# Row maxima inside the last value projections, the values of a head in one group, and three banks for scores, in an attention and mixture-of-experts layer

## What is computed

```python
q = _split_heads(hidden_states @ Wq + bq)   # 2 batches, 16 heads of 32
k = _split_heads(hidden_states @ Wk + bk)
v = _split_heads(hidden_states @ Wv + bv)
ctx = _local_attention(q, k, v)             # 8 blocks of 128 queries, each over 256 keys around it
idx = _global_index(q)                      # token 0, the 62 largest |q|, token 1023
qg = jnp.take_along_axis(q, idx[..., None], axis=-2)
g_scores = jnp.einsum('nhqd,nhkd->nhqk', qg, k) / math.sqrt(d)
g_ctx = jnp.einsum('nhqk,nhkd->nhqd', jax.nn.softmax(g_scores, axis=-1), v)
ctx = ctx.at[bn, bh, idx].set(g_ctx)
...
x = x + _layernorm(_L0_attn_ref(_layernorm(x), ...))
x = x + _layernorm(_L0_ffn_ref(_layernorm(x), ...))   # 8 experts, top 1, and a shared expert
```

## Time and profile before

| what | value |
|---|---|
| median of 3 runs (lowest, highest) | 936.01 us (935.06, 940.03) |
| profiled execution: its time | 939.68 us |
| profiled execution: its span | 937.9 us |
| PE busy | 854.9 us, 91% |
| DVE busy | 579.7 us, 62% |
| ACT busy | 412.6 us, 44% |
| mean granted PE clock | 0.957 of full speed |

### The profile page before, as it was taken

One profiled execution on the slowest core, in us unless ns is written; L12 is line 12 of the kernel. 1 busy time (PEld: TensorE's weight loads), 2 busy tenths in 40 slices (PEclk: granted clock), 3 DMA queues, 4 the chain that ended last, 5 costly groups with the idle time before them and its releaser, 6 DMA issues.

```text
span 937.9 us, 13768 instructions
## 1 busy us (share of the span) xinstructions
PE 854.9 (91%) x5094; PEld 681.8 (73%) x5094; DVE 579.7 (62%) x1236; ACT 412.6 (44%) x771; POOL 135.8 (14%) x189
## 2 busy tenths in 40 slices
PE   3999999978899899999879999989999999999995
PEld 2676776756566666666658778779999999877773
DVE  5636994668745554656448754436666677648565
ACT  2523241215446555555544424346666666633120
POOL 4000003020030000111113552100000000012222
PEclk9999999969989999999979889989999999999997
DMA  6696554973656855762025862256666667645434
GB/s 202 180 331 193 165 158 143 268 198 90 183 153 170 199 130 159 185 195 79 14 70 195 277 230 82 89 161 206 209 210 203 201 212 208 209 134 164 156 124 134
DMA packets 116642, 161.07 MB, mean 172 GB/s; under 512 B 17156, under 2 KB 65028, under 8 KB 116576
## 3 DMA queue, kind: packets, MB, share of 16 engines
q1 hardware_dynamic: 112992, 152.23, 53.8%
q0 software_dynamic: 3584, 7.97, 3.0%
HBM read 105.93 MB, written 55.05 MB: 172 GB/s over the span
## 4 chain that ended last, share of the span: by engine, by line
PE 75%; DVE 13%; ACT 5%; DMA 3%; issue 2%; POOL 1%; SPq 1%; DVEq 0%; POOLq 0%
PE bank L162 43%; PE wide L162 24%; PE wide L166 4%; PE bank L166 3%; DVE SG L159 2%; ACT PG L156 2%; DMA H<-scr_oe,FG 1%; DMA scr_v<-vt 1%; DVE XT L148 1%; DVE STC L266 1%; DVE CX L1320 1%; DVE MX L159 1%; DVE W13L L148 1%; ACT PT L156 1%; DVE SIL L148 1%
## 5 line engine op out<-in xcount | busy, mean ns | idle before, releaser
L162 PE MATMUL bank<-XT,W13H 128*128 128x256 f32 (+1 forms) x1056 | 246.2, 328 | 3.1 <-DVE XT L148 3.1
L162 PEld LDWEIGHTS bank<-XT,W13H 128*128 128x128 f32 x1056 | 177.1, 193 | 22.1 <-issue 3.2
L162 PE MATMUL bank<-XT,W13L 128*128 128x256 f32 (+1 forms) x528 | 171.0, 324 | 0.0
L162 PE MATMUL wide<-W2H,HH 128*128 128x512 f32 (+1 forms) x384 | 130.4, 409 | 2.9 <-DVE CX L1320 2.9
L159 DVE TENSOR_REDUCE MX<-wide 128x1 f32<-128x192 f32 (+1 forms) x128 | 77.8, 651 | 52.6 <-PE wide L162 52.6
L162 PEld LDWEIGHTS bank<-XT,W13L 128*128 128x128 f32 x528 | 101.5, 192 | 8.4
L162 PEld LDWEIGHTS wide<-W2H,HH 128*128 128x128 f32 (+1 forms) x384 | 74.8, 195 | 26.4 <-DVE CX L1320 4.6
L148 DVE TENSOR_TENSOR SIL<-bank,SIL 128x256 f32<-128x256 f32 (+1 forms) x72 | 36.9, 512 | 80.8 <-ACT SIL L156 80.2
L162 PE MATMUL bank<-HT,WH 128*128 128x512 f32 x256 | 84.8, 413 | 2.1 <-DVE HT L148 1.6
L156 ACT ACTIVATE PT<-bank 128x512 f32<-128x512 f32 x128 | 74.3, 595 | 26.9 <-PE bank L162 25.8
L156 ACT ACTIVATE SIL<-bank 128x256 f32<-128x256 f32 (+1 forms) x72 | 32.7, 454 | 115.5 <-PE bank L162 114.6
(11 more groups left out here) (186 smaller groups left out, 1450.0 us busy)
## 6 DMA issues: line engine op xcount, KB each, us to landing
R<-in_L_ffn_W_dram SPq DMA_DIRECT2D x48, 512.0 KB, 5.1
scr_q<-hl SPq DMA_DIRECT2D x16, 512.0 KB, 4.2
scr_k<-hl SPq DMA_DIRECT2D x16, 512.0 KB, 3.9
late<-scr_q SPq DMA_DIRECT2D x60, 128.0 KB, 3.2
late<-scr_k SPq DMA_DIRECT2D x60, 128.0 KB, 3.5
R<-in_L_ffn_sw_dram SPq DMA_DIRECT2D x12, 512.0 KB, 5.0
QSe<-scr_q SPq DMA_DIRECT2D x36, 128.0 KB, 4.3
KSe<-scr_k SPq DMA_DIRECT2D x36, 128.0 KB, 4.6
```

Of the source, the lines that this page charges most:

```text
L162: return do("pe", lambda g: g.matmul(ps, a, b, start=start, stop=stop, skip_group_check=True), after, mark=mark)
```

## The change

1. `row_max` of heads 0 and 1 moves into `proj_group`: a new function `first_maxima(j)` runs behind the value tile j of the last group, and always on `wide2`. Behind j = 0 it also loads heads 2 and 3, into the space of the high Q and K weights, which are separate tiles for that. `row_shift(0)` stands behind j = 3, `row_shift(1)` and `stack_q(0)` at g = 1. In period 0 all global steps are one slot later (`late`).
2. `local_values` of a head's four units stands in one group, at k = 0 and 4.
3. `ST_` has three banks, `O_` one.
4. `global_back` writes into a bank of ST_, and the W_ buffer is free once ACT has copied it to OS.
5. `MX` is 72 columns wide and zeroed by POOL at the start; the transpose takes all 72 columns. `PT` has six buffers.

```diff
+        for b in MX.bufs:
+            m_mxz = do("pool", lambda g, b=b: g.memset(b[:, :], 0.0), [m_kfirst])
...
+                    if g4 == 3:
+                        first_maxima(j)
                 HT.busy[hti].append(m_p)
+            def first_maxima(j):
+                if j == 0:
+                    m_last = Q_last(Q, "pe")
+                    W_.busy[1] = tp.busy[0] + tp.busy[1]
+                    for r, w in ((QS, WQK[0][0]), (KS, WQK[1][0])):
+                        for h in range(2):
+                            r.bufs.append(w[0:97, 2 * h:2 * h + 2, :].rearrange("p k n -> p (k n)"))
+                            r.busy.append([m_last])
+                            r.slots.append(slot())
...
+                    load_head(2, kv_b0)
+                    load_head(3, kv_b0)
+                if j == 3:
+                    row_shift(0, W_, 1)
+                row_max(j // 2, j % 2, 1)
...
-            MX = ring("MX", 4, [P, NB])
...
-            ST_ = Ring(banks[0:2], first=fence_ps)
-            O_ = Ring(banks[2:4], first=fence_ps)
+            W_.busy[0] = list(fence_ps)
+            ST_ = Ring(banks[0:3], first=fence_ps)
+            O_ = Ring(banks[3:4], first=fence_ps)
...
-                g_["m_t"] = tr(g_["w"][:, 512:512 + 2 * VW], os[0:2 * VW, 0:P], ident[0:2 * VW, 0:2 * VW], [m_c, m_id], mark=True)
+                ti, tb, tfree = ST_.take()
+                g_["back"] = (ti, tb)
+                g_["m_t"] = tr(tb[:, 0:2 * VW], os[0:2 * VW, 0:P], ident[0:2 * VW, 0:2 * VW], [m_c, m_id] + tfree, mark=True)
...
-                W_.busy[g_["wi"]].append(m_f)
+                ST_.busy[ti].append(m_f)
...
-            load_head(2)
-            load_head(3)
-            for n in range(2):
-                row_max(n, 0)
-                row_max(n, 1)
-                row_shift(n)
-            stack_q(0)
...
+                    if g == 1:
+                        row_shift(1, ST_)
+                        stack_q(0)
+                    if k == 1 + late:
                         global_scores(i)
...
-                if g >= 2 and g % 2 == 0:
-                    local_values((g - 2) // 4, (g - 2) % 4)
-                    local_values((g - 2) // 4, (g - 1) % 4)
+                if g >= 4 and g % 4 == 0:
+                    for u in range(4):
+                        local_values(g // 4 - 1, u)
```

More of the change, by code:

```diff
@@ L207, in sandwich @@
         VS0 = [sb(early, "VSe", [P, 9, 4 * VW])]
+        WQK = [[sb(early, f"W{a}{h}", [P, 4, D], F32R) for h in "HL"] for a in "QK"]
+        MX = Ring([sb(early, f"MX{i}", [P, 72]) for i in range(4)])
+        MR = Ring([sb(early, f"MR{i}", [NB, P], F32R) for i in range(4)])
+        W_ = Ring([wide, wide2])
         k0 = do("pool", lambda g: g.memset(ident[:, :], 0.0))
@@ L348, in load_v, with row_max, row_shift @@
             vq[m] = dict(i=vi, v=vb, m=mv)
+        row_slots = [slot() for _ in range(6)]
+        def row_max(n, u, at=None):
+            hd = heads[n]
+            wi, wb, wfree = W_.take(at)
+            if u == 0:
+                hd["mi"], hd["mx"], hd["mfree"] = MX.take()
+                hd["mfree"].append(m_mxz)
+            mx, mfree = hd["mx"], hd["mfree"]
+            for a in range(4):
+                i = 4 * u + a
+                lo, hi = max(0, 128 * i - 64), min(SEQ, 128 * i + 192)
+                c0 = a * 256 + (64 if i == 0 else 0)
+                m_s = mm(wb[:, c0:c0 + hi - lo], hd["q"][0:96, i * P:(i + 1) * P], hd["k"][0:96, lo:hi],
+                         True, True, [hd["mq"], hd["mk"]] + wfree, mark=(a == 3))
+            if u == 0:
+                a1 = red(mx[:, 0:1], wb[:, 64:256], ALU.max, [m_s] + mfree)
+                a2 = red(mx[:, 1:4], wb[:, 256:1024].rearrange("p (a c) -> p a c", a=3), ALU.max, [m_s])
+            else:
+                a1 = red(mx[:, 4:7], wb[:, 0:768].rearrange("p (a c) -> p a c", a=3), ALU.max, [m_s])
+                a2 = red(mx[:, 7:8], wb[:, 768:960], ALU.max, [m_s])
+            W_.busy[wi].append(a2)
+            hd["m_mx"] = a2
+        def row_shift(n, ring, at=None):
+            hd = heads[n]
+            ti, tb, tfree = ring.take(at)
+            m_t = tr(tb[0:72, 0:P], hd["mx"][:, :], ident[:, :], [hd["m_mx"], m_id] + tfree, mark=True)
+            MX.busy[hd["mi"]].append(m_t)
+            ri, rw, rfree = MR.take()
+            m_c = copy("act", rw[:, :], tb[0:NB, 0:P], [m_t] + rfree)
+            ring.busy[ti].append(m_c)
+            qb = hd["q"]
+            hd["m_row"] = dma("sp", row_slots[hd["qi"]], lambda g: g.dma_start(
+                f(qb[96:97, :]).rearrange("o (b q) -> o b q", q=P), f(rw[:, :])), [m_c])
+            MR.busy[ri].append(hd["m_row"])
         with ExitStack() as st:
@@ L721, in sandwich @@
             ct, ctx_stored, gp = {}, {}, {}
[L723 to L749, removed]
-                MX.busy[hd["mi"]].append(m_t)
-                ri, rw, rfree = MR.take()
-                m_c = copy("act", rw[:, :], tb[0:NB, 0:P], [m_t] + rfree)
-                ST_.busy[ti].append(m_c)
-                qb = hd["q"]
-                hd["m_row"] = dma("sp", Rows[hd["qi"]], lambda g: g.dma_start(
-                    f(qb[96:97, :]).rearrange("o (b q) -> o b q", q=P), f(rw[:, :])), [m_c])
-                MR.busy[ri].append(hd["m_row"])
-            Rows = row_slots
             UNITS = (((1, 0, 0, 256), (5, 512, 256, 512)),
```

52 lines of the change are left out of this document (27 added, 25 removed).

## The result

The changed kernel takes 949.9 us (median of 4 executions, 946.53 to 951.91) against 937.75 us (4 executions, 935.06 to 940.03): ratio 1.0127, 95% interval 1.0082 to 1.0172. It is slower; the forecast was no change. The profiled execution took 949.15 us, with a span of 947.4 us, 9.5 more than before, and its mean granted clock is 0.945 instead of 0.957.

The account below looks back on a forecast made before the run. PE was taken as the bound, so only its waits could be won. Terms -4.9 - 0.8 + 2.0 + 1.7 + 1.5 + 0.5 summed to 0.0, giving 936.0 us, no change; 8-in-10 range 927 to 942 us.

Parts of the forecast that it names:

- The turn's wait takes the place of the work that hid it: First global turn of a plain period: PE still waits for PG, some 1.05 us instead of 0.57, with values gone.
- What is late next at this place is nothing: First row maximum of a period: once its 1.0 us wait for GC goes, no other wait replaces it.
- The -0.8 for these periods: Periods 1 and 2, where DVE is late: the bank saves 0.5 us each, less 0.24 once; -0.8 us together.
- the +2.0 for FD: Period 2: values ahead of the search-rows wait, then values at half clock, cost +2.0 us (bound +0.2).
- -0.50 (bank) - 1.0 (GC) + 0.99 (values uncovered) = -0.5 us: One plain period: third bank and earlier buffer release save, values moved out of the turn's wait cost; -0.5 of 15.8 us.
- my own sign, plain periods under 15 us: Attention loop: plain periods expected at 15.3 us; under 15 us would show the main step wrong.
- -4.9: Ten plain intervals between global turns together: a gain of 4.9 us (bound 3.3).
- The seam, +1.5: Last value projections to loop: clock falls at a 2.4 us gap, +1.5 us; full clock at 200 us would disprove it.
- +0.5 for the start: Kernel start: POOL clears four MX tiles ahead of the first layer-norm scale, +0.5 us (bounds 0 and 0.9).
- `stack_q(1)` and the end, +1.7: Period with `stack_q(1)` +0.7, period 15 +0.1, last head's values at loop end +0.9; +1.7 us together.
- The wider transpose, 0: Weight loads of 72 columns: at most 58 ns more, 32 times, costed at 0 because they run beside the row maximum.
- the third: Rival: low clock lasts from the seam over the first period, to near 218 us; slower, 941 us; chance 0.15.

Follow-up runs that it names:

- the release alone: Kernel before, with only the global rows turned back into a value bank, so ACT's copy frees the wide buffer: 940.54 us, ratio 0.9949.
- experiments 1: Changed kernel plus five unused matmuls of 512 columns ahead of the global turn's wait for PG: 945.78 us, ratio 1.0023 to the kernel before.
- 3: The seam alone: changed kernel's new seam with the loop of the kernel before: 946.74 us, ratio 1.0045 to the kernel before.
- experiment 9: Changed kernel with the values in pairs of units again at every even slot, all else kept: 939.13 us, ratio 1.001 to the kernel before.
- the loop alone: Kernel before with only the changed loop (values grouped, three score banks, one value bank, early buffer release), old seam: 951.11 us, ratio 1.0100.

## Why the prediction was wrong

- **The turn's wait takes the place of the work that hid it** ("some 1.05 us instead of 0.57"): right, 1.24 us, with the start 3.75 us after the global scores as worked out.
- **"What is late next at this place is nothing"**, for GC: right in plain periods. In periods 1 and 2 it was wrong: the time saved at GC came back in the waits behind it (in period 1, 0.83, 1.26 and 0.71 us for GC, MX and PT became 1.47 for MX and 1.40 for PG, in the release alone 2.33 for MX), and the clock fell there. The -0.8 for these periods and the +2.0 for FD measured +6.3 together. The FD wait itself is 2.17 us, as forecast.
- **The failed step is the sum of a plain period, "-0.50 (bank) - 1.0 (GC) + 0.99 (values uncovered) = -0.5 us".** Its waits were right and its size at full clock was even too small, -1.0: a group of twenty value matmuls takes 1.86 us to the next start, where twelve and eight took 1.99, and 1.2 is left for GC. So by my own sign, plain periods under 15 us, the step was wrong at full clock already, on the good side. (Ten times that sum, -0.51, is -5.1 and not -4.9; it changes nothing.) But it priced the uncovered values at their length and left the clock where it was. I asked of the seam and of period 2 what an emptied wait does to the clock, from the earlier trace rows, and never of the wait that returns fifteen times. In four of the ten plain periods only that fell, at +1.6 us each, and in a fifth a DMA was late as well (19.03 us): 0.0 for the ten instead of -4.9.
- **The seam, +1.5 and +0.5 for the start:** +0.4 in the profiled execution, with period 0; the start itself is +0.35. I let the clock fall in the projections behind the 2.4 us wait; here the wait was 2.08 us and the clock was 1.00 until 201 us, so by my own sign this step was wrong. That the first global scores came 2.3 us later, near the +2.0, was luck. In experiments 1, 3 and 9 it did fall there behind the same wait, and with that the first global scores of 1 and 3 came at 211.1 and 211.0 us. Over ten executions the seam alone costs 0.45%, 4.2 us, with an interval from 0.9 to 7.5 us, so my 2.0 isn't refuted. How much of it is the clock and how much the waits for MX, for the row DMA and for GS stays open.
- **`stack_q(1)` and the end, +1.7:** +3.5, again with low clock, at 303.5 to 307 us and at the end.
- **The wider transpose, 0:** right. The load of 72 columns took 117 ns, 34 more than one of 8, and its group had no idle time. The Trainium skill, TensorE: Matmul & The Clock Gate, in LDWEIGHTS (loading the stationary operand), gives load time in proportion to the columns. The estimate worked out from it in the prediction, 53 ns more for 64 columns, was too high here, where 34 were measured.
- **The rivals:** the third, at 0.15, was on the right side and named the clock, but put it in period 0, which became 1.9 us shorter. That the clock falls in the plain periods was no rival at all.

How much of it is the clock? Over the 25 executions of the kernel before on one chip, a microsecond of clock loss goes with 0.84 us of time; over 13 on each of two others, with 0.81 and 0.73. The profiled executions of before and after differ by 52.1 - 40.3 = 11.8 us of clock loss, an estimate of 9 to 10 of their 9.5 us. That it comes out so closely is chance: the feed-forward part was at the lower level for 37 us before and for 20 after, and is only 0.7 us shorter, while between 200 and 500 us there are 42 us more. A microsecond of low clock isn't worth the same everywhere. For the loop alone it is 58.9 - 39.5 = 19.4 us, an estimate of 14 to 16 where 9 were measured; so at an equal clock the changed loop would by this estimate be some 5 to 7 us faster than before, near the -4.9 of the forecast's plain periods (its whole loop was -2.0). Together with experiments 1 and 9 this shows the clock as the main cause in the loop. It is not shown which activity before a wait decides: the same 1.24 us were followed by full clock in one period and by half in the next.

## What to carry to other kernels

A wait on a busy PE can have two prices, its length and what the clock does behind it. Before work is moved out of a wait that recurs, ask what is left around the wait, and compare the change with a version in which unused matmuls fill it: if that is faster, the clock is what you pay for. Where another engine is the limit of a stretch, a stall removed on PE comes back in the next one; spread that engine's work first (here 1.5% with the release), then remove the stall.

## What was unexpected of the hardware

- The clock fell behind waits of 1.24 us in a loop in which PE was otherwise busy, in some periods and not in others with the same instructions. The Trainium skill, TensorE: Matmul & The Clock Gate, in HAM oscillation — how this bites in real kernels, describes a clock that falls again and again in the waits between short groups of matmuls, with waits for DMAs of some 3 to 5 us. The trace agrees in kind and not in length: here 1.24 us were enough.
- Fifteen waits of 1.0 to 1.5 us, 1.1 on average, with values behind them (experiment 9) left the clock up in all ten plain periods.
- Executions of one kernel differ by their clock: the ten of experiment 9 lie between 933.35 us at a mean clock of 0.966 and 945.21 us at 0.949.
